# A gated slot-attention block with a SwiGLU on one Trainium2 core: key-state products moved ahead of the key projection, and the queue's stores and loads put in another order

## The reference

```python
x = x + attn(layernorm(x))          # x is (4, 512, 512)
x = x + ffn(layernorm(x))
# attn, 16 heads, 64 slots, key width 64, value width 128:
q, k, v, s = heads(h @ Wq), heads(h @ Wk), heads(h @ Wv), clip(heads(h @ Ws), -32, 32)
z = cumlogsumexp(s, time); g = exp(z[t-1] - z[t]); p = exp(s - z)
hk[t] = hk[t-1] * g[t] + k[t] (x) p[t];  ok[t] = (q[t] / 8) . hk[t]
hv[t] = hv[t-1] * g[t] + p[t] (x) v[t];  o[t] = softmax(ok[t]) . hv[t]
o = o * rsqrt(mean(o^2) + eps) * g_norm_weight * silu(h @ Wg);  return o @ Wo
# ffn: weights rounded to float8_e4m3fn, silu(gate) * up, then down, each times its scale
```

## Time and profile before

| what | before |
|---|---|
| median of 3 runs (lowest to highest) | 1340.43 us (1340.0 to 1342.96) |
| the profiled execution's own time | 1341.52 us |
| its span, first to last instruction | 1339.8 us |
| PE busy | 1323.1 us, 99% |
| DVE busy | 1057.4 us, 79% |
| ACT busy | 428.2 us, 32% |
| POOL busy | 137.3 us, 10% |
| mean granted clock of PE | 0.999 |
| DMA: mean share of 16 engines, q1 | 48.2%, 149.37 MB |

### The profile page before, as it was taken

How to read it: one execution, slowest core, us unless ns; L and a number is a source line. 1 busy time by engine, 2 the same in 40 slices (tenths; PEclk the granted TensorE clock), 3 DMA queues, 4 the chain that set the end, 5 groups by cost and what they waited for, 6 DMA issues and landing times.

```text
span 1339.8 us, 24318 instructions
## 1 busy us (share of the span) xinstructions
PE 1323.1 (99%) x9303; PEld 1099.2 (82%) x9303; DVE 1057.4 (79%) x1684; ACT 428.2 (32%) x1287; POOL 137.3 (10%) x106
## 2 busy tenths in 40 slices
PE   8999999999999999999999999999999999999998
PEld 7887888788878888888888888878888888888887
DVE  8888888888878888888888888888778776755454
ACT  5433323332323233323323332333233333232221
POOL 3001101110111012001200210011010010000000
PEclk9999999999999999999999999999999999999999
DMA  6157555655665566556555655566442564120000
GB/s 189 40 116 176 113 117 121 163 122 117 137 147 119 111 148 136 120 117 155 133 128 115 162 127 134 119 151 136 85 107 44 155 165 87 47 49 31 0 32 32
DMA packets 532241, 150.88 MB, mean 113 GB/s; under 512 B 385185, under 2 KB 523297, under 8 KB 532129
## 3 DMA queue, kind: packets, MB, share of 16 engines
q1 hardware_dynamic: 532128, 149.37, 48.2%
HBM read 88.95 MB, written 60.36 MB: 111 GB/s over the span
## 4 chain that ended last, share of the span: by engine, by line
PE 72%; DVE 10%; SPq 7%; DMA 7%; issue 3%; ACT 1%; DVEq 0%; ACTq 0%
PE bank L493 14%; PE bank L118 13%; PE bank L495 12%; PE bank L494 12%; PE bank L1789 6%; SPq L372 4%; PE bank L735 3%; SPq L336 2%; PE bank L718 2%; DMA fp_weights<-q 2%; PE bank L583 2%; DMA e_tokens<-k_tok_then_wT 2%; PE bank L563 2%; DMA k_tok_then_wT<-w_slots 1%; PE bank L723 1%
## 5 line engine op out<-in xcount | busy, mean ns | idle before, releaser
L493 PE MATMUL bank<-wvg_hi,xT_hi 128*128 128x512 f32 x512 | 206.7, 404 | 0.7
L495 PE MATMUL bank<-wvg_hi,xT_lo 128*128 128x512 f32 x512 | 199.9, 390 | 0.0
L494 PE MATMUL bank<-wvg_lo,xT_hi 128*128 128x512 f32 x512 | 199.8, 390 | 0.0
L828 ACT ACTIVATE a_and_v<-bank 128x256 f32<-128x256 f32 x128 | 49.0, 383 | 324.7 <-PE bank L495 324.6
L493 PEld LDWEIGHTS bank<-wvg_hi,xT_hi 128*128 128x128 f32 x512 | 96.2, 188 | 25.0 <-issue 3.6
L495 PEld LDWEIGHTS bank<-wvg_hi,xT_lo 128*128 128x128 f32 x512 | 96.1, 188 | 20.6
L494 PEld LDWEIGHTS bank<-wvg_lo,xT_hi 128*128 128x128 f32 x512 | 96.3, 188 | 17.8
L1170 DVE RECIPROCAL cT<-cT 128x512 f32<-128x512 f32 x32 | 107.0, 3342 | 0.0
L1115 POOL TENSOR_TENSOR rstd<-ssq,neg_half 128x8 f32<-128x8 f32 x32 | 52.4, 1637 | 506.0 <-DVE ssq L1218 506.0
L493 PE MATMUL bank<-wo_hi,oT_hi 128*128 128x512 f32 x256 | 99.8, 390 | 0.0
L495 PE MATMUL bank<-wo_hi,oT_lo 128*128 128x512 f32 x256 | 99.6, 389 | 0.0
(11 more groups left out here) (180 smaller groups left out, 3045.8 us busy)
## 6 DMA issues: line engine op xcount, KB each, us to landing
o_transposed<-o SPq DMA_DIRECT2D x27, 512.0 KB, 3.5
oT_lo<-o_transposed SPq DMA_DIRECT2D x108, 128.0 KB, 3.1
fp_weights<-q SPq DMA_DIRECT2D x28, 318.0 KB, 3.3
e_tokens<-k_tok_then_wT SPq DMA_DIRECT2D x31, 256.0 KB, 2.3
e_tok<-e_tokens SPq DMA_DIRECT2D x124, 64.0 KB, 2.3
c_tokens<-cT SPq DMA_DIRECT2D x31, 256.0 KB, 2.4
cT<-c_tokens SPq DMA_DIRECT2D x124, 64.0 KB, 2.3
w_slots<-p SPq DMA_DIRECT2D x27, 256.0 KB, 2.4
```

Of the source, the lines that this page charges most:

```text
L493: pe.matmul(dst, w_hi, m_hi, start=(k == 0), stop=False)
L494: pe.matmul(dst, w_hi, m_lo, start=False, stop=False)
L495: last = pe.matmul(dst, w_lo, m_hi, start=False, stop=(k == n - 1))
L828: return act.activation(dst, src, ACT.Copy)
```

## The change

On PE the inter-chunk products become `inter_ok(u)`, called right after the hv parts, ahead of KTJ, and `inner_ok` is cut into two halves with a key sum behind each. On ACT the exp of the softmax (`slot_exp`) comes ahead of the copy of the keys (not in unit 0), and `split_vg` ahead of the key-state copies. On DVE `far_lo` (or `out_lo`) comes after the subtraction, and `lo_vg` ahead of the clip. On SP `load_w` comes ahead of `load_e`, `load_skq(pair, 2)` ahead of `store_o`, and `store_q8` ahead of the loads of i = 1; the wait of `load_e` is on the hv parts instead of the key sums. The lines are those of the kernel before.

```diff
@@ -241,7 +241,7 @@
     ffn.place(projected=s_job, out_w_read=s_wl, weights_split=s_vgh, vg_lo=(s_vgl, s_vgl2), q_read=s_ok,
-              k_read=s_kb, scores=s_a, e_read=s_hkd, weights_done=s_b, w_ready=s_wm, inter_done=s_oi,
+              k_read=s_kb, scores=s_a, e_read=s_hvd, weights_done=s_b, w_ready=s_wm, inter_done=s_oi,
               w_transposed=s_trw, gated=s_oev, gates=s_g, out_transposed=s_tro, out_done=s_y, added=s_ya,
@@ -393,7 +393,7 @@
             sp.wait_ge(s_est, 16 * nu)
-            sp.wait_ge(s_hkd, (CH - 1) * nu)
+            sp.wait_ge(s_hvd, nu)
             load_blocks(e_tok[:, :, :].rearrange("t c m -> t (c m)"), e_dram, s_eld)
@@ -425,6 +425,7 @@
 
+            sp.wait_ge(s_est, 16 * (u + 1))
             sp.wait_ge(s_wst, 16 * (far_before(u) + 1))
@@ -462,14 +463,13 @@
                 store_w(u)
+                load_w(u)
             load_e(u + 1)
-            if u in W_FAR:
-                load_w(u)
+            if i == 2:
+                load_skq(pair, 2)
             if u - 1 <= FAR:
...
             store_k(u + 1)
-            if i == 2:
-                load_skq(pair, 2)
             if i == 3:
@@ -479,10 +479,10 @@
             load_c(u + 1)
+            store_q8(u)
             if i == 1:
...
                 load_vg(pair)
-            store_q8(u)
 
@@ -583,6 +583,18 @@
 
+        def inter_ok(u):
+
+            pe.wait_ge(s_hk, 3 * (u + 1))
+            for c in range(1, CH):
+                for a in range(2):
+                    hs = slice(DK * a, DK * (a + 1))
+                    for h in range(2):
+                        ts, ds = slice(64 * h, 64 * (h + 1)), slice(c * P + 64 * h, c * P + 64 * (h + 1))
+                        mm = pe.matmul(ok_of[a][c][ts, :], qT[hs, ds], hk[hs, c - 1, :],
+                                       start=False, stop=True, skip_group_check=True)
+            mm.then_inc(s_ok, 1)
+
         def out_transposes(u, banks):
@@ -645,15 +657,17 @@
             pe.wait_ge(s_v, (u + 1) * CH)
-            inner_ok(par, range(CH))
+            inner_ok(par, (0, 1))
             key_sums(u, 1)
+            inner_ok(par, (2, 3))
+            key_sums(u, 2)
             for c in range(CH - 1):
...
             mm.then_inc(s_hvd, 1)
-            key_sums(u, 2)
+            inter_ok(u)
             if u > FAR + 1:
@@ -673,15 +687,6 @@
                 mm.then_inc(s_trc, 1)
-            pe.wait_ge(s_hk, 3 * (u + 1))
-            for c in range(1, CH):
-                for a in range(2):
-                    hs = slice(DK * a, DK * (a + 1))
-                    for h in range(2):
-                        ts, ds = slice(64 * h, 64 * (h + 1)), slice(c * P + 64 * h, c * P + 64 * (h + 1))
-                        mm = pe.matmul(ok_of[a][c][ts, :], qT[hs, ds], hk[hs, c - 1, :],
-                                       start=False, stop=True, skip_group_check=True)
-            mm.then_inc(s_ok, 1)
             if not first:
@@ -923,6 +928,11 @@
 
+        def slot_exp(u):
+
+            act.wait_ge(s_sub, u + 1)
+            act.activation(p[:, :], p[:, :], ACT.Exp).then_inc(s_exp, 1)
+
         def wT_evac(u):
@@ -936,6 +946,10 @@
                 norm_hi(0, (2, 3))
+            if i == 3 and not tail:
+                act.wait_ge(s_job, job_count(VG3, u, i))
+                for k in range(KT):
+                    split_vg(pair_of_next(u), k)
             for c in range(CH - 1):
@@ -949,17 +963,14 @@
                 far_hi(u - 2)
-            if i == 3 and not tail:
-                act.wait_ge(s_job, job_count(VG3, u, i))
-                for k in range(KT):
-                    split_vg(pair_of_next(u), k)
+            if not first:
+                slot_exp(u)
             if not last:
...
                 copy(c_tok, A[0][:, :]).then_inc(s_ctok, 1)
-            act.wait_ge(s_sub, u + 1)
-            act.activation(p[:, :], p[:, :], ACT.Exp).then_inc(s_exp, 1)
+                slot_exp(u)
             if last:
@@ -1323,6 +1334,9 @@
                 norm_lo(0, (2, 3))
+            if i == 3 and not tail:
+                for k in range(2):
+                    lo_vg(pair_of_next(u), k)
             if not last:
@@ -1331,11 +1345,6 @@
             value_states(u)
-            if u > FAR + 1:
-                out_lo(u - 1, A)
-            elif u > 1:
-                far_lo(u - 2)
-
             p3 = p[:, :].rearrange("p (s m) -> p s m", m=M)
@@ -1352,6 +1361,10 @@
                               ALU.subtract).then_inc(s_sub, 1)
+            if u > FAR + 1:
+                out_lo(u - 1, A)
+            elif u > 1:
+                far_lo(u - 2)
             v = product_of(u)
@@ -1367,9 +1380,6 @@
                 o_turn(u - 1)
-            if i == 3 and not tail:
-                for k in range(2):
-                    lo_vg(pair_of_next(u), k)
             if last:
@@ -1716,7 +1726,7 @@
         sp.wait_ge(w["k_read"], UNITS - 1)
-        sp.wait_ge(w["e_read"], (CH - 1) * UNITS)
+        sp.wait_ge(w["e_read"], UNITS)
         load_down(2)
```

## The result

The changed kernel takes 1330.9 us in the median of four runs (1329.12 to 1331.66), against 1341.7 (1340.0 to 1344.89) for the kernel before, measured beside it. The ratio is 0.9912, with a 95% interval of 0.9896 to 0.9928. Forecast were 1324.5 and 17.2 us against this median; 10.8 were gained. The profiled executions are 12.4 us apart (spans of 1339.8 and 1327.4; 1341.52 and 1329.12 with what lies around them); that of the changed kernel was the fastest of its four.

The account below looks back on a forecast made before the run. PE's own queue was taken to bound the kernel (busy 1323.1 of 1339.8 us). A 6.2, B 8.1 and C 1.7 sum to 16.0: 1325.5 for a like execution, 1324.5 for the median, range 1317.6 to 1335.

Parts of the forecast that it names:

- excess of 11.56 us: PE, units 2 to 27: time beyond 25 undisturbed units of 32.23 us; 9.3 in i == 2, 2.3 in i == 3.
- Part A: PE's f32 block: inter-chunk products moved behind the hv products save one passage, 0.20 us per unit, 6.2 us (0 to 10.9).
- 0.11 as saved at the last key sum: PE: the last key sum takes 0.22 ahead of the key job, the one ahead of the hv products 0.11.
- The passage: PE: going from three-product matmuls to small f32 ones and back; one fewer was to save 0.35 us per unit.
- the closeness of the copies: PE key sums wait for ScalarE's copy of the one before, with less work between: two stalls, 0.15 us per unit.
- The release: Time from another engine's end to PE's next matmul, about 0.10 us, read at VectorE's value-weight split.
- rival 1: Key-state copies bound PE's f32 block: two stalls of 0.17 or more, A gives nothing, 1330.7 us; chance 0.15.
- Part B: w load in i == 2 units: pulled forward 3.2 us, it ends PE's w_slots waits; 8.1 us (4 to 9.3).
- the price at Ws: i == 2 units: the fp8 store ahead of the Ws load makes Ws land later; 1.2 us over seven units.
- Part C: i == 3 units: sooner value-weight splits end the 0.38 us hold of the VG0 job; 1.7 us (-1.5 to 2.7).
- two holds of 0.88: i == 3 units: POOL's splits hold VectorE's norm and delay oT_lo; one 0.88 us hold covered, two not quite.
- Rival 4: oT_lo behind the subtraction overruns 1.7 us of slack and delays the output product in every unit; 1351.4 us, chance 0.05.

Follow-up runs that it names:

- the balanced run: Changed kernel with the f32 block reordered so each key-state copy has more PE work ahead of what waits for it; 1326.5 us, ratio 0.9882.
- both mends: Changed kernel with the f32 block reordered and the attention output's low half ahead of the maximum in the last unit; 1324.75 us, ratio 0.9857.

## Why the prediction was right or wrong, point by point

**What bounds the kernel: right.** All that was gained went out of PE's queue: PE is busy in all of the stretch now, and of its excess of 11.56 us some 0.5 are left (804.13 against 25 x 32.145).

**Part A, 6.2 us forecast, 26 x 0.085 = 2.2 measured** in units 2 to 27: the step that failed. Its mechanism held (the key and the query job are 0.11 and 0.13 shorter), but two terms of the sum were mis-sized. I counted 0.11 as saved at the last key sum, and nothing as added. The key sum no longer stands ahead of the big products, but the step from the hv to the inter-chunk products is new, and there the balanced run shows 0.10 with no copy to wait for. The passage was not spared, it moved. And I put the closeness of the copies at 0.15; the balanced run puts it at 0.165, of which part is the key sums themselves, 0.17 instead of 0.12 behind a wait. 0.11 + 0.13 - 0.165 = 0.075, near the 0.085. The release I took from the earlier trace rows (0.10) was too long here; from the end of a copy to the next key sum are 0.05. The forecast was right that rival 1 was near: of the 0.24 that were saved, two thirds are given back.

**Part B, 8.1 forecast, 8.9 measured.** The w load ahead of the e load does nearly all of it by itself, and with the wait the stretch at a lowered clock went: cut into windows of 4 us, all of the stretch of the changed kernel has a granted clock of 1.00, where the earlier trace rows had 0.61 in 383 to 387. The forecast took 1.2 us for the price at Ws, and it was nearly nothing in the traced execution: unit 6 takes 32.16, and all seven units with i = 2 together have 0.4 of excess, 0.24 of it in unit 26. That was close and not room to spare. The slack of 0.87 in unit 6 became 0.22, that of the other six, 1.5 to 2.4 before, became 0.10 to 1.0, and with both mends one such unit lost 1.35. The forecast's mechanism was right, and that it cost nothing here is in part luck.

**Part C, 1.7 forecast, 2.4 measured.** The port held VectorE as the rule and the earlier trace rows said, both halves of the norm, but by 1.27 us together and not by two holds of 0.88, and the 1.7 us of slack covered it. But this gain is not the splits' own in the changed kernel: the matmul order alone had already emptied it (excess of i = 3 from 2.6 to 0.1).

**The parts are not additive.** Alone, the matmul order gave 8.6 us of the stretch (817.31 to 808.67), the queue's order 8.5, the splits 4.4; together they gave 13.2. And oT_lo behind the subtraction costs 0.94 us in each unit with PE's old order. With the new one it gains at most 5.8 us in the stretch of one slow traced execution, and nothing that the times show. I had priced each part against the kernel before only.

**Rival 4** came true in one unit, the last, for 1.07 us of wait and 1.3 in all, and its sign was the one foretold, a new row of waits for oT_lo. I had laid its slack out for ordinary units and not asked what is different in the one unit without a query job. That is a third miss.

**The sum.** By the profiled executions 16.0 were forecast and 12.4 found, 3.6 fewer: 4.0 from part A and 1.1 from the rest (1.3 lost in the last unit, 0.2 to 0.3 won by part A in the last four), less the 1.5 that B and C gave over their terms. The forecast missed the median by 6.4 (1330.9 against 1324.5). The other 2.8 of it are no step of the change: I took 1.0 off for the median, and the changed kernel's median lies 1.8 above its profiled execution (1329.12). Inside the stated range the forecast was some 6 us too hopeful; that B and C came out above their terms hid part of the miss in A.

## What to carry to other kernels

When a step is moved in PE's queue to spare a passage, look whether the passage is spared or only moved, and price each change of tile shape inside the block like one. Where a chain goes through another engine's copy, count the work that PE has between the two, and split the consumers by which copy they need. Before moving a step behind a wait on a second engine, find the unit in which the wait is longest, the first and the last above all. After a move in a DMA queue, measure the slack of what was pushed back: no list of waits shows it until it is used up, and then it appears under another name.

## What the runs showed that I had not expected

- Going from f32 matmuls on 128 rows to those on 64 rows took PE 0.10 us more between starts, with no copy to wait for, about as much as the 0.11 for leaving the big products.
- A key sum that comes behind a short wait took 0.17 between starts instead of 0.12.
- Ws took 4.8 and 4.9 us from issue to landing right behind the fp8 store, and 3.0 to 3.2 without the store ahead of it. The slack of the output product, two engines further on, shrank by about as much.
- After an idle stretch of 1.88 us PE ran at a mean granted clock of 0.61 for 4 us, which cost 1.6 us more. After one of 1.80 in unit 2 (a wait for w_slots at 121 us) and one of 2.28 in the head (at 23 us) of the same execution it stayed at 1.00, and so it did after the stalls of 0.68 in the run with the old matmul order. The length of a stall alone does not tell what it costs.
- The start of unit 2 varied from 97.0 to 101.1 us between traces, 97.0 to 98.8 of it between two kernels that differ only in the last unit.
